# LoRA inputs built in transposed form from the split x, eight-column gates and a reordered start in a gated cross-attention + MoE kernel

## The reference, cut to what matters

```
x = x + tanh(g_xattn) * attention(ctx, layernorm(x), b, seq_len)     # 16 heads of width 8
n = layernorm(x)
scores = softmax(n @ gate_w.T + gate_b)                              # 8 experts
top_v, top_i = top_k(scores, 2)
for e in range(8):
    gate  = (number of times e is in top_i) * sum(top_v)
    inter = n @ wi.T + bi + (n @ lora_A[e].T) @ lora_B[e].T          # rank 16, 512 columns
    out  += gate * (relu(inter) @ wo.T + bo)
x = x + tanh(g_ffn) * out
```

## Time and profile before

| | |
|---|---|
| median of 3 runs | 277.94 us |
| profiled execution, its own time | 278.2 us |
| its span, first to last instruction | 276.4 us |
| TensorE matmul busy | 245.5 us (89%) |
| VectorE busy | 214.0 us (77%) |
| ScalarE busy | 163.0 us (59%) |
| GpSimd busy | 158.5 us (57%) |
| granted TensorE clock | full speed throughout |

### The profile page before, as it was taken

How to read it: one execution, slowest core, us unless ns; L and a number is a source line. 1 busy time by engine, 2 the same in 40 slices (tenths; PEclk the granted TensorE clock), 3 DMA queues, 4 the chain that set the end, 5 groups by cost and what they waited for, 6 DMA issues and landing times.

```text
span 276.4 us, 8038 instructions
## 1 busy us (share of the span) xinstructions
PE 245.5 (89%) x2966; PEld 184.3 (67%) x2966; DVE 214.0 (77%) x623; ACT 163.0 (59%) x319; POOL 158.5 (57%) x306
## 2 busy tenths in 40 slices
PE   0368979899998999989999979999999999999895
PEld 0135556566665566656567658888888989897865
DVE  4778786899999999997949999858585858585432
ACT  5778785889897989896877642333334242323220
POOL 6888676687877786686892447090919250505120
PEclk9999999999999999999999999999999999999999
DMA  4749997736776866640000000101010101001011
GB/s 110 202 124 209 208 222 181 206 83 196 178 215 160 215 160 162 149 71 6 8 6 2 4 0 0 39 2 38 0 40 0 42 0 30 10 7 31 2 38 38
DMA packets 48461, 23.46 MB, mean 85 GB/s; under 512 B 7680, under 2 KB 48296, under 8 KB 48424
## 3 DMA queue, kind: packets, MB, share of 16 engines
q1 hardware_dynamic: 47520, 22.77, 34.5%
q10 hardware_dynamic: 904, 0.19, 0.4%
HBM read 7.29 MB, written 2.10 MB: 34 GB/s over the span
## 4 chain that ended last, share of the span: by engine, by line
PE 57%; DVE 24%; POOL 5%; ACT 5%; issue 5%; DMA 2%; ACTq 1%; POOLq 0%
PE bank L1102 21%; DVE negmax L1313 11%; PE bank_max L1137 10%; PE bank L1012 7%; PE bank L1044 5%; PE bank L1079 2%; DVE rest L1264 2%; PE bank L1055 2%; PE bank L1095 2%; PE bank L1018 2%; DMA b_rows<-in_L_xattn_b_dram 2%; DVE hsum L1440 2%; ACT stack L760 2%; DVE KV L1326 1%; PE bank L1068 1%
## 5 line engine op out<-in xcount | busy, mean ns | idle before, releaser
L1313 DVE TENSOR_REDUCE negmax<-bank 128x4 f32<-128x512 f32 x128 | 83.3, 680 | 10.7 <-PE bank L1012 10.6
L809 ACT ACTIVATE probs<-bank 128x512 f32<-128x512 f32 x128 | 71.7, 602 | 15.0 <-PE bank L1018 13.9
L1012 PE MATMUL bank<-stack 64*128 64x128 bf16 x512 | 51.9, 235 | 9.6 <-DVE negmax L1313 6.0
L1012 PEld LDWEIGHTS bank<-stack 64*128 64x128 bf16 x512 | 31.7, 101 | 31.2 <-DVE negmax L1313 19.8
L1102 PE MATMUL bank<-u_part,b_part 128*128 128x512 f32 x192 | 52.0, 399 | 0.1
L849 ACT ACTIVATE h<-bank,bi_col 128x512 f32<-128x512 f32 x32 | 22.1, 690 | 49.4 <-PE bank L1102 49.4
L1018 PE MATMUL bank<-stack 64*128 64x128 bf16 x512 | 48.5, 223 | 0.3
L1440 DVE SCALAR_TENSOR_TENSOR hsum<-bank,nbi_col,h 128x512 f32<-128x512 f32 x32 | 23.9, 748 | 24.0 <-PE bank L1102 24.0
L648 POOL TENSOR_TENSOR x_part<-KV,x_part 128x512 fp32r<-128x512 f32 x8 | 10.4, 1301 | 55.8 <-ACT x_part L831 55.8
L1044 PE MATMUL bank<-probs,vpad 128*32 128x128 f32 x1024 | 42.1, 283 | 0.0
L1102 PEld LDWEIGHTS bank<-u_part,b_part 128*128 128x128 f32 x192 | 35.5, 189 | 8.3 <-ACT h L849 0.5
(11 more groups left out here) (136 smaller groups left out, 407.0 us busy)
## 6 DMA issues: line engine op xcount, KB each, us to landing
stack<-part SPq DMA_DIRECT2D x96, 128.0 KB, 3.0
KV<-in_ctx_dram SPq DMA_DIRECT2D x5, 512.0 KB, 4.1
X<-in_x_dram SPq DMA_DIRECT2D x7, 256.0 KB, 4.3
out_dram<-res SPq DMA_DIRECT2D x7, 256.0 KB, 2.3
KV<-in_ctx_dram SPq DMA_DIRECT2D x5, 256.0 KB, 5.6
...
```

What stands on the lines that cost most here:

```text
L809: act.activation(probs[:, i % 4, :], sc2[i % 2][:, :], ACT.Exp).then_inc(s_exp, 1)
L1012: mm = pe.matmul(sc1[i % 2][:, j * 128:(j + 1) * 128], stack[at, s, h0 + 2 * j, q0:q0 + 128], stack[at, s, h0 + 2 * j, 512 + q0:640 + q0], ...
L1313: dve.tensor_reduce(negmax[:, p % 2, n % 2, 8 * (u // 2) + u % 2:8 * (u // 2) + u % 2 + 7:2], bank_cols(sc1[i % 2]), AX.X, ALU.max, negate ...
```

## The change

1. LoRA values are computed as `ag_part` (loaded) times `x_part` (512 columns moving) by `three` in fp32r, in bank 1, so that the LoRA rows lie in partitions at once (`lora`). The eight gate columns are computed alone (`gate_logits`), in bank 0, with the transposed x still the loaded operand.
2. The masks are widened to 128 columns by GpSimd in bf16 (`widen_masks`) and transposed by TensorE (`transpose_masks`, eight bf16 transposes). VectorE multiplies the two parts of the LoRA values with them (`mask_u(g, k)`, two operations of 512 elements for each k). The LoRA values are split before the masking, once (`u_high`, `u_low`).
3. `agT` is split as well (`ag_part`, one ScalarE and one GpSimd operation, once). Waits and positions are moved to suit.
4. At the start `b_rows` is first in ScalarE's queue, two of the `seq_col` loads go to SyncE's, `bias_to_stack(0)` goes from SyncE's queue to ScalarE's; the addition of the bias comes after `bias_places`; `first_rest(0)` and `third_part(0)` come earlier on VectorE; `place_bias(2)` and `copy_line(2)` come earlier, and `transpose_k(2)` and `transpose_q(2)` after the first scores.

Buffers, semaphores and the counter `NGATE` (21 to 20) are left out here:

```diff
-        def ug_bank(t):
-
-            return bank[t // 2]
+        def gate_cols():
+
+            return bank[0][:, 0:GT * E]
+
+        def u_bank():
+
+            return bank[1][:, :]
...
-        def u_banks(g):
-
-            return (qk_t[:, :], bank_out) if g == 0 else (qk_t[:, :], o_t[:, :])
+        def mask_bank(g):
+
+            return bank_max[:, :] if g == 0 else o_t[:, :].bitcast(BF16)
...
             load_x(0)
             load_k(0)
+            for i in range(1, PARTS):
+                sp.dma_start(seq_col[B * i:B * (i + 1), :], seq_len).then_inc(s_col, 16)
             load_x(1)
...
             pair_to_stack(0, 0)
             pair_to_stack(0, 1)
-            bias_to_stack(sp, 0)
             pair_to_stack(0, 2)
...
+            def bias_add():
+
                 pool.wait_ge(s_bias, 1)
                 pool.wait_ge(s_b, 16)
                 pool.tensor_tensor(bias_rows[:, :], mask_rows[:, :], b_rows[:, :], ALU.add).then_inc(s_bias, 1)
...
+            def lora_low():
+                pool.wait_ge(s_wTc, 7)
+                pool.tensor_tensor(ag_part[:, 1, :], agT[:, 0:E * R], ag_part[:, 0, :], ALU.subtract).then_inc(s_w_lo, 1)
+
+            def widen_masks(g):
+                pool.wait_ge(s_gate, NGATE * (g + 1))
+                if g >= 1:
+                    pool.wait_ge(s_hotT, g)
+                pool.tensor_copy(hot_wide[:, :, :, :].rearrange("p k t (e r) -> p (k t e) r", r=R),
+                                 hot[:, 0:2, :, :].rearrange("p k t e -> p (k t e)")[:, :, None].to_broadcast([128, 2 * GT * E, R])
+                                 ).then_inc(s_hot, 1)
...
             power(0)
             bias_sum()
             bias_places()
+            bias_add()
             bias_split()
...
+                    lora_low()
                 if q == PAIRS:
                     x_low(0)
                     rsqrt2(2)
                     normalise2(2)
                 if q == PAIRS + 1:
+                    widen_masks(0)
+                if q == PAIRS + 2:
                     rsqrt2(3)
                     normalise2(3)
+                    x_low(1)
...
             for g in range(GROUPS):
                 if g + 1 < GROUPS:
-                    x_low(g + 1)
+                    widen_masks(g + 1)
                 make_base(g)
                 if g + 4 < GROUPS:
                     rsqrt2(g + 4)
                     normalise2(g + 4)
+                if g + 2 < GROUPS:
+                    x_low(g + 2)
...
         def _(act):
-            for i in range(PARTS):
-                act.dma_start(seq_col[B * i:B * (i + 1), :], seq_len).then_inc(s_col, 16)
+            act.dma_start(b_rows[:, :], b.rearrange("(o k) -> o k", o=1).to_broadcast([PARTS * B, S])).then_inc(s_b, 16)
+            act.dma_start(seq_col[0:B, :], seq_len).then_inc(s_col, 16)
             act.dma_start(seq_row[:, :], seq_len.rearrange("b o -> o b").to_broadcast([128, B])).then_inc(s_seq, 16)
-            act.dma_start(b_rows[:, :], b.rearrange("(o k) -> o k", o=1).to_broadcast([PARTS * B, S])).then_inc(s_b, 16)
...
+                if i == 3:
+                    act.activation(ag_part[:, 0, :], qk_t[:, 0:E * R], ACT.Copy).then_inc(s_wTc, 1)
...
+            def u_high(g):
+                act.wait_ge(s_uT, g + 1)
+                if g >= 1:
+                    act.wait_ge(s_u, 4 * g)
+                act.activation(u_whole[:, 0, :], u_bank(), ACT.Copy).then_inc(s_u_hi, 1)
...
             copy_line(0)
+            bias_to_stack(act, 0)
             normalise_first(1)
...
             bias_to_stack(act, 1)
+            copy_line(2)
             load_gates()
             first_part(2)
...
+                        if at == (0, 1, 3):
+                            u_high(0)
                         if at == (1, 1, 3):
-                            copy_uT(0)
+                            x_high(1)
...
                 if g + 2 < GROUPS:
                     copy_xT(g + 2)
                 relu(g, 1)
-                if g + 1 < GROUPS:
-                    x_high(g + 1)
                 relu(g, 2)
                 relu(g, 3)
                 if g + 1 < GROUPS:
-                    copy_uT(g + 1)
+                    u_high(g + 1)
                 if g + 2 < GROUPS:
+                    x_high(g + 2)
                     gate_exp(g + 2)
...
                 if g == 0:
                     pe.wait_ge(s_shift, 3)
-                    pe.wait_ge(s_wTc, 6)
-                elif g == 1:
-                    pe.wait_ge(s_xTc, 1)
-                elif g >= 2:
-                    pe.wait_ge(s_u_lo, 2 * g - 3)
+                    pe.wait_ge(s_wTc, 7)
+                else:
+                    pe.wait_ge(s_xTc, g)
                 for t in range(GT):
                     mm = pe.transpose(qk_t[:, t * 128:(t + 1) * 128], spare(g)[:, t, :], ident[:, :])
                 mm.then_inc(s_xT, 1)
...
-            def lora_and_gates(g):
+            def gate_logits(g):
                 pe.wait_ge(s_xTc, g + 1)
-                if g >= 1:
-                    pe.wait_ge(s_u, 4 * g)
+                if g == 0:
+                    pe.wait_ge(s_max, CH * B)
                 else:
-                    pe.wait_ge(s_max, CH * B)
+                    pe.wait_ge(s_gate, NGATE * (g - 1) + 1)
                 for t in range(GT):
-                    c0 = (t % 2) * UW
-                    mm = pe.matmul(ug_bank(t)[:, c0:c0 + UW], spare(g)[:, t, :], agT[:, :],
+                    mm = pe.matmul(gate_cols()[:, t * E:(t + 1) * E], spare(g)[:, t, :], agT[:, E * R:UW],
                                    start=True, stop=True)
                 mm.then_inc(s_ug, 1)
...
+            def lora(g):
+                pe.wait_ge(s_x_lo, g + 1)
+                if g == 0:
+                    pe.wait_ge(s_w_lo, 3)
+                    pe.wait_ge(s_max, CH * B)
+                else:
+                    pe.wait_ge(s_u_lo, g)
+                three(u_bank(), [ag_part[:, k, :] for k in range(2)],
+                      [x_part[:, g % 2, k, :] for k in range(2)], True, True).then_inc(s_uT, 1)
+
+            def transpose_masks(g):
+                pe.wait_ge(s_hot, g + 1)
+                if g == 0:
+                    pe.wait_ge(s_mTc, PAIRS)
+                elif g == 1:
+                    pe.wait_ge(s_norm, NNORM * PAIRS)
+                else:
+                    pe.wait_ge(s_u, 4 * g)
+                for k in range(2):
                     for t in range(GT):
-                        mm = pe.transpose(dst[:, t * 128:(t + 1) * 128],
-                                          u[:, i, t, :, :].rearrange("p e r -> p (e r)"), ident[:, :])
-                    mm.then_inc(s_uT, 1)
+                        at = 512 * k + 128 * t
+                        mm = pe.transpose(mask_bank(g)[:, at:at + 128], hot_wide[:, k, t, :], identb[:, :])
+                mm.then_inc(s_hotT, 1)
...
                 if c == 0:
-                    pe.wait_ge(s_u_lo, 2 * g + 1)
+                    pe.wait_ge(s_u, 4 * g + 2)
...
                 if c == 0:
-                    pe.wait_ge(s_u_lo, 2 * g + 2)
+                    pe.wait_ge(s_u, 4 * g + 4)
...
             place_bias(1)
-            transpose_k(2)
-            transpose_q(2)
+            place_bias(2)
...
                         scores(m, n, c)
+                        if (q, i, c) == (0, 0, 0):
+                            transpose_k(LEAD)
+                            transpose_q(LEAD)
...
                         if at == (0, 0, 1):
-                            lora_and_gates(0)
+                            gate_logits(0)
                         if at == (0, 0, 2):
                             transpose_x(1)
+                        if at == (0, 1, 1):
+                            lora(0)
+                        if at == (1, 0, 2):
+                            gate_logits(1)
                         if at == (1, 1, 1):
-                            transpose_u(0)
-                        if at == (1, 1, 2):
-                            lora_and_gates(1)
+                            transpose_masks(0)
                         if at == (2, 1, 0):
-                            pe.wait_ge(s_w_lo, 2)
                             first_expert(0, 0)
...
                 first_expert(g, 3)
                 second_expert(g, 2)
                 if g + 1 < GROUPS:
-                    transpose_u(g + 1)
+                    lora(g + 1)
                 second_expert(g, 3)
                 if g + 2 < GROUPS:
-                    lora_and_gates(g + 2)
+                    gate_logits(g + 2)
+                if g + 1 < GROUPS:
+                    transpose_masks(g + 1)
                 out_weights(g)
...
             dve.tensor_copy(slot_words(0, 2), word_of(2)).then_inc(s_ones[0], 1)
+            first_rest(0)
             moments_of(1)
-            first_rest(0)
+            third_part(0)
             scale(1)
-            for n in range(4, 6):
-                stats_of(n)
-            third_part(0)
-            for n in range(6, 8):
```

(47 more changed lines are left out.)

62 lines of the change are left out of this document (19 added, 43 removed).

## The result

The changed kernel takes 281.24 us (median of 4 runs, 280.58 to 282.70), the kernel before 277.78 (277.12 to 278.81) beside it: ratio 1.0121, 95% interval 1.0086 to 1.0155. It is 3.5 us slower by the medians. The forecast was 279.3 with a range of 276.3 to 280.9, so the time lies outside it; the sign was the likelier one of the forecast's chances by a hair (0.42 for slower, 0.41 for same). The profiled execution of after took 280.58 us with a span of 278.8 (before: 278.2 and 276.4).

What follows compares the result with a forecast made beforehand. TensorE was taken to bound the steady groups, VectorE the change of phase, full DMA engines 17.2 to 38.2. Start -0.9, phase +1.2, groups +1.2, seam -0.17 gave +1.3 on 277.94: 279.3 us, range 276.3 to 280.9.

Steps and rivals of the forecast that it cites:

- The start: Program start up to the DMA train: pair 1's second part and the train come 0.9 us earlier, bounds -1.8 and +0.3.
- the bound for a late `seq_col`: Upper bound of the start: +0.3 us if `seq_col` is late, with its part on SyncE's queue.
- The 0.1 for `bias_to_stack(0)`: ScalarE's queue at the start: 0.1 us or so lost, as it stands between `copy_line(0)` and `normalise_first(1)`.
- The change of phase: About 143 to 171 us: VectorE's wait and added work delay the first sum by 1.7, net +1.2 us, bounds -0.1 and +2.3.
- it has slack: Change of phase: TensorE waits about 1.3 us at `transpose_o` for `add_attention(14)`, but has slack until `sum_experts(0,0)`.
- Steady groups: TensorE in the tail: lora, masks and gates added, 1.80 removed, +0.23 us a group, +1.2 for groups 1 to 5.
- the seam: After group 6: 0.84 us with or without the masks; `lora` replaces `transpose_u` there, -0.17 us.
- The gates shrink with their columns: Rival, chance 0.18: in the gates loads hide, eight short matmuls take 0.45 us or less; total 276.6 or 276.3.
- GpSimd late with the masks: Rival, chance 0.05: a widening takes 3 us or more, VectorE waits 1.5 longer at `mask_u(0)`; 280.8 and beyond.
- No wait at the masks: Rival, chance 0.15: in the change of phase ScalarE and TensorE hide all the wait; 277.0, up to 278.
- The start is given back: Rival, chance 0.17: at SyncE's queue at 38.2 ScalarE binds and the 0.9 us gain is absorbed; 280.2.

Runs made afterwards that it cites:

- start_only: The kernel before with the new start alone (small loads, order of mask and bias work, bias transfer): 280.57 us beside 278.17, ratio 1.0082.
- lora_only: The changed kernel with the old start, so only the new lora inputs, masks and gates: 279.61 us, ratio 1.0031 to the kernel before.

## Why the forecast was wrong, step by step

- **The start: -0.9, bounds -1.8 to +0.3. It was +2.4**, and this step alone is 3.3 us of error, more than the miss of 1.9. The sentence that failed is "With that `power(1)` and the normalisation of pair 1 come about 1.0 earlier": `power(1)` came 1.5 later and the normalisation 2.5 later. And the bound for a late `seq_col` was set at 0.3 without a row. I followed `b_rows` out of the chain, rightly, and didn't ask which load would end last then: `seq_col`, cast at 6.9 in place of 4.0, ahead of `mask_rows` and the bias rows on GpSimd. The 0.1 for `bias_to_stack(0)` on ScalarE's queue was 0.64, since its issue took 1.59 and not the 0.49 of a plain one. That `first_rest(0)` ahead of `moments_of(1)` makes `power(1)` wait for the statistics had no term.
- **Given back in the attention:** -1.5 in the profile, in no term; start_only has 0.3 of it. 0.95 of it is the moment at which the clock rises, which is found early and late in profiles with and without the change. 0.26 comes ahead of the ninth `row_max`, as in the four other profiles with a part of the new start and in none of the rest; the last 0.26 has no source that I can show.
- **The change of phase: +1.2. It was +1.5**, and the mechanism was right up to the addition. VectorE's wait for the masks was 1.05 (forecast 1.3), the first sum slipped by 1.9 (1.7). Wrong was "it has slack": the slip of `add_attention(14)` made TensorE idle 2.58 (1.3) and then run at the lower level, 0.92 granted over 150 to 171. No term had the pace behind a gap. With the executions of before and lora_only as above, it seems to be most of what this half of the change costs in the medians.
- **Steady groups: +0.23 each. It was +0.02.** Lora inputs 0.70 as priced (7.70 for 33 where the earlier trace rows has 6.29 and 0.70), masks 0.46 (0.45). Gates 0.79 (0.88): 0.112 for a load, as read out of the earlier trace rows, but seven such loads and not eight, the first lying beside the matmul ahead. `out_weights` 3.63 in place of 3.76, which I hadn't priced. 0.70 + 0.46 + 0.79 - 0.13 - 1.80 = +0.02. Together with the seam, groups 1 to 6 cost nothing (+2.44 to +2.41) where I had +1.0.
- **Rivals.** "The gates shrink with their columns" is refuted: 8 and 128 columns keep one pace. The Trainium skill, "TensorE: Matmul & The Clock Gate", section "LDWEIGHTS (loading the stationary operand)", gives 107 ns for a load of 128 columns, and the trace agrees with 0.109 to 0.112 from start to start. "GpSimd late with the masks" is refuted too: a widening took 1.085 on average, the nearest row had said 1.50. "No wait at the masks" is refuted by VectorE's 1.05. "The start is given back" assumed a gain that didn't exist.
- **The sum.** By profiles +2.4 for 278.2 to 280.58: 2.44 - 1.47 + 1.47 - 0.03. By medians 3.5, of which the two halves measured alone give 2.3 for the start and 0.9 for the rest; the 0.95 from the pace, which this one profile had and a median need not have, would explain most of the difference to the profiles, which isn't shown.
